# Scan steps, transpositions and layer 4 in another order in the second half of a macaron block

## What is computed

```python
x = x + 0.5 * ffn(layernorm(x))        # first half
x = x + attn(layernorm(x))             # a recurrence in place of attention
x = x + 0.5 * ffn(layernorm(x))        # second half, the same weights

def ffn(x):                            # widths 128, 512, 512, 512, 128
    h = silu(x @ w1.T * s1) * (x @ w2.T * s2)
    h = gelu(h @ h1.T * t1)
    h = gelu(h @ h2.T * t2)
    return h @ w3.T * s3

def attn(x):                           # 16 states
    xB = x @ B
    h_t = tanh(xB_t + h_(t-1) @ A.T)   # scanned over 512 positions
    return (h @ C) @ W_out.T + b_out
```

## Time and profile before

| what | value |
|---|---|
| median of 3 runs | 382.91 us |
| the profiled execution | 382.39 us |
| its span (first to last instruction) | 380.4 us |
| TensorE busy | 373.4 us (98%) |
| VectorE, ScalarE, GpSimd busy | 280.2 (74%), 261.0 (69%), 177.6 us (47%) |
| TensorE's granted clock over the span | 0.996 |

### The profile page before, as it was taken

The page is one execution under the profiler, slowest core; times in us unless marked ns, Lnnn a source line. Parts: engine busy times, 40 slices in busy tenths (PEclk is TensorE's granted clock), DMA queues, the critical chain, the costliest instruction groups (busy, mean ns, idle before and its releaser), DMA issues.

```text
span 380.4 us, 6512 instructions
## 1 busy us (share of the span) xinstructions
PE 373.4 (98%) x1773; PEld 297.2 (78%) x1773; DVE 280.2 (74%) x711; ACT 261.0 (69%) x605; POOL 177.6 (47%) x161
## 2 busy tenths in 40 slices
PE   7999999999999999999999999999999999999995
PEld 6877777878788787878778788888888888887774
DVE  5978988887787977677968876767867677786713
ACT  3889485667758678675684767858576785857653
POOL 2645265575746558342452623535233353533421
PEclk9999999999999999999999999999999999999998
DMA  7920010102001020000001000010100001010001
GB/s 235 434 108 1 28 57 28 57 2 83 3 28 56 2 83 0 28 1 29 28 2 55 3 28 28 2 55 1 55 0 27 28 0 55 0 52 7 2 28 32
DMA packets 7805, 16.64 MB, mean 44 GB/s; under 512 B 1888, under 2 KB 2912, under 8 KB 7520
## 3 DMA queue, kind: packets, MB, share of 16 engines
q1 hardware_dynamic: 6768, 16.01, 11.2%
q10 hardware_dynamic: 1008, 0.29, 0.3%
HBM read 9.99 MB, written 2.12 MB: 32 GB/s over the span
## 4 chain that ended last, share of the span: by engine, by line
PE 96%; ACT 2%; issue 0%; DVE 0%
PE F L288 75%; PE FR L288 8%; PE SC L504 2%; PE FR L316 1%; PE F L541 1%; PE SC L436 1%; PE F L532 1%; PE MI L316 1%; PE MI L296 1%; PE FR L306 1%; PE SC L288 1%; PE F L534 1%; PE SC L451 1%; ACT y_hi L1235 1%; PE MI L458 0%
## 5 line engine op out<-in xcount | busy, mean ns | idle before, releaser
L288 PE MATMUL F<-y_hi,w_hi 128*128 128x512 f32 (+1 forms) x484 | 196.9, 407 | 0.3 <-DVE y_lo L1059 0.2
L288 PE MATMUL F<-y_lo,w_hi 128*128 128x512 f32 (+1 forms) x484 | 188.4, 390 | 0.0
L288 PEld LDWEIGHTS F<-y_hi,w_hi 128*128 128x128 f32 x484 | 91.0, 188 | 24.0 <-issue 6.0
L1232 ACT ACTIVATE y<-F,sc 128x512 f32<-128x512 f32 x111 | 76.0, 685 | 43.1 <-PE F L288 41.9
L288 PEld LDWEIGHTS F<-y_lo,w_hi 128*128 128x128 f32 x484 | 91.2, 188 | 15.3
L853 DVE TENSOR_TENSOR y_lo<-y,y_hi 128x512 fp32r<-128x512 f32 x79 | 66.3, 839 | 39.9 <-ACT y_hi L1235 39.9
L1506 POOL TENSOR_TENSOR y_lo<-y,y_hi 128x512 fp32r<-128x512 f32 x48 | 66.6, 1394 | 58.7 <-DVE y_hi L840 48.1
L1512 POOL TENSOR_TENSOR y_lo<-y,y_hi 128x512 fp32r<-128x512 f32 x48 | 62.5, 1309 | 35.1 <-ACT y_hi L1235 35.1
L1235 ACT ACTIVATE y_hi<-F,sc 128x512 fp32r<-128x512 f32 x111 | 75.9, 684 | 0.0
L1251 ACT ACTIVATE h<-SC 128x32 fp32r<-128x32 f32 x96 | 18.8, 195 | 49.3 <-PE SC L451 48.3
L288 PE MATMUL F<-xn_hi,w_hi 128*128 128x512 f32 x118 | 49.4, 419 | 0.0
(11 more groups left out here) (177 smaller groups left out, 438.8 us busy)
## 6 DMA issues: line engine op xcount, KB each, us to landing
w_raw<-mr_row SPq DMA_DIRECT2D x5, 512.0 KB, 3.4
x_all<-in_xT SPq DMA_DIRECT2D x1, 2048.0 KB, 16.2
x_all<-x1c SPq DMA_DIRECT2D x8, 256.0 KB, 2.3
x_all<-lnin SPq DMA_DIRECT2D x8, 256.0 KB, 2.2
out<-outb SPq DMA_DIRECT2D x7, 256.0 KB, 2.0
x_all<-in_xtok SPq DMA_DIRECT2D x1, 1536.0 KB, 12.1
w_raw<-in_h1T SPq DMA_DIRECT2D x2, 512.0 KB, 7.7
w_raw<-in_h2T SPq DMA_DIRECT2D x2, 512.0 KB, 9.0
```

The costliest lines, as they stand in the source:

```text
L288: mm = nc.tensor.matmul(out, wtile(w, layer, k, m), y, start=first and i == 0, stop=last and i == len(pairs) - 1)
L1232: nc.scalar.activation(y23[:, m, :], bankt[:, :], ACT.Gelu, scale=s)
```

## The change

It moves calls within three streams. On TensorE, `middle_turn` has steps 3, 4, 6 and 7 of the second pass at other products of layer 3. `turn` has step 0 inside layer 4, `front_tokens` one product ahead of layer 4's end, step 1 ahead of layer 2 block 1, step 2 and `to_features` inside layer 2 block 2, step 3 ahead of layer 2 block 3, and step 5 behind layer 1 block 2 instead of ahead of it. For this `layer4` takes a function that it calls behind each product, and its signal is given inside the loop. VectorE and ScalarE get the steps 0 to 3, `front` and the low part of layer 2's block 1 in an order that follows. ScalarE's part from step 4 on stays as it was; so do GpSimd and SyncE.

```diff
--- before.py
+++ after.py
@@ -383,7 +383,7 @@
                         mm.then_inc(l3_mm, 1)
                     beside(k)
 
-            def layer4(g, gen):
+            def layer4(g, gen, beside=lambda k: None):
                 if isinstance(g, int) and g == 0:
                     pe.wait_ge(y3_hi_r, 3)
                 else:
@@ -395,7 +395,9 @@
                     else:
                         pe.wait_ge(y3_lo_dve, (KT - 1) * g + k)
                     mm = split_mm(B4[:, :], 4, k, 0, y3_hi[:, k, :], y3_lo[:, k, :], k == 0, k == KT - 1, gen)
-                mm.then_inc(l4_mm, 1)
+                    if k == KT - 1:
+                        mm.then_inc(l4_mm, 1)
+                    beside(k)
 
             def last_layer3(g, ms, ks, gen):
 
@@ -624,11 +626,11 @@
                 layer3(g, 0, gen, lambda k: x_times_b(mid) if k == 1 else step(0) if k == KT - 1 else None)
                 layer1(g + 1, 2, gen)
                 step(1)
-                layer3(g, 1, gen, lambda k: step(2 + k // 2) if k % 2 else None)
-                layer3(g, 2, gen, lambda k: step(4 + k // 2) if k % 2 else None)
+                layer3(g, 1, gen, lambda k: step(2) if k == 1 else None)
+                layer3(g, 2, gen, lambda k: step(3 + k // 2) if k % 2 == 0 else None)
+                step(5)
                 layer1(g + 1, 3, gen)
-                step(6)
-                layer3(g, 3, gen, lambda k: step(7) if k == 1 else None)
+                layer3(g, 3, gen, lambda k: step(6 + k // 2) if k % 2 == 0 else None)
 
             def last_turn(g, r, gen):
                 layer2(g, 0, gen, lambda i: layer4(g - 1, gen) if i == 2 else None)
@@ -648,28 +650,32 @@
                     if scan is not None:
                         scan_step(scan[0], scan[1], t)
 
-                def opening(i):
-                    if att is not None and i == 1:
+                def within_layer4(k):
+                    if k == 1:
+                        step(0)
+                    if k == 2:
+                        front_tokens(g + 1)
+
+                def opening(k):
+                    if att is not None and k == 1:
                         attention(att[0], att[1])
-                    if i == 2:
-                        if joined:
-                            layer4(g - 1, gen)
+                    if k == 2 and joined:
+                        layer4(g - 1, gen, within_layer4)
+                    if k == 2 and not joined:
+                        step(0)
                         front_tokens(g + 1)
                 layer2(g, 0, gen, opening)
-                step(0)
+                step(1)
                 layer2(g, 1, gen)
-                step(1)
-                layer2(g, 2, gen)
-                step(2)
-                to_features("f", xnt_f, FR, g + 1)
+                layer2(g, 2, gen, lambda k: step(2) if k == 0 else to_features("f", xnt_f, FR, g + 1) if k == 2 else None)
+                step(3)
                 layer2(g, 3, gen)
-                step(3)
                 layer1(g + 1, 0, gen)
                 layer1(g + 1, 1, gen)
                 step(4)
                 layer3(g, 0, gen)
+                layer1(g + 1, 2, gen)
                 step(5)
-                layer1(g + 1, 2, gen)
                 layer3(g, 1, gen)
                 step(6)
                 layer3(g, 2, gen)
@@ -1017,16 +1023,16 @@
                 if att is not None:
                     attention(att[0], att[1])
                 low1(g)
+                step(0)
                 front_stats(g + 1)
                 if joined:
                     layer4(1, g - 1, k - 1)
-                step(0)
                 step(1)
                 normalise("f", g + 1, FR, mv_f, rs_f, xnt_f)
+                step(2)
                 low(g, 1, y2_hi_r, y23, y2_hi, y2_lo, y2_lo_dve)
-                step(2)
+                step(3)
                 xn_low(g + 1)
-                step(3)
                 low(g, 3, y2_hi_r, y23, y2_hi, y2_lo, y2_lo_dve)
                 first_gates(g + 1, step, (4, None, 5, None))
                 step(6)
@@ -1350,12 +1356,11 @@
                 if scan is not None:
                     inject(scan[0], scan[1])
                 step(0)
+                step(1)
                 gelu2(g, 0)
-                step(1)
-                gelu2(g, 1)
-                step(2)
-                gelu2(g, 2, lambda: front(g + 1))
-                step(3)
+                gelu2(g, 1, lambda: step(2))
+                front(g + 1)
+                gelu2(g, 2, lambda: step(3))
                 gelu2(g, 3)
                 layer1(g + 1, 0)
                 layer1(g + 1, 1)
```

## The result

The changed kernel takes 388.99 us (median of 5 runs, 388.02 to 389.48) against 382.57 (5 runs, the three known before among them; 382.18 to 382.96): a ratio of 1.0171, interval 1.0156 to 1.0185. That is 1.1 us over the forecast of 387.9 and inside the range. Against the kernel before, 6.4 us were added where 5.0 were forecast: 1.4 more. The time misses by only 1.1 because the kernel before came out 0.34 lower than the 382.91 on which the forecast stood. The profiled executions are 389.48 us with a span of 387.4, and 382.39 with 380.4: 7.0 us apart, of which 0.4 arose before the middle turns, where the kernels are the same.

What follows compares the result with a forecast made beforehand. TensorE, 96% of the chain, was taken to bound the kernel. Loop turns 3.6, turn 1 0.6, turn 6 0.37 and middle turns 0.4 gave 5.0 on 382.39, 387.4; with 0.52 to the median, 387.9 us, range 383.7 to 389.6.

Steps and rivals of the forecast that it cites:

- the main term: Step 5 behind layer 1 block 2 delays `th`, the gate and layer 3 block 2: 0.49 us lost in each of five turns.
- A+3.46: TensorE's load for layer 3 block 2, 3.46 us after A, the start of layer 1 block 2; TensorE ready at A+2.98.
- the second transposition: On TensorE, waiting for `xnt_f` from VectorE and GpSimd: a loss between 0 and 0.23 us, taken as 0.10.
- layer 1 block 0: On TensorE, waiting for `xn_lo` behind step 3: 0.15 late plus 0.10 for the load, 0.25 us; 0.10 outside the loop.
- F+0.70: End of `xn_hi`, 0.70 us (0.66 and 0.04) after F, the second transposition, on the way to `xn_lo` at F+3.07.
- Turn 1: The turn whose waits use constants: losses 0.49, 0.10, 0.10 and 0.15 less 0.23 won, +0.6 us.
- Turn 6: Turn without scan: the chain to the second transposition starts 0.09 sooner, two matmuls (0.46) stand behind its end: +0.37 us.
- Middle turns: Steps 3, 6 and 7 win 0.15 us, step 5 loses 0.28: net +0.13, three times, 0.4 us.
- rival 3: ScalarE and VectorE don't catch up: `lnin` 0.2 later in five turns, attention waits 0.13 three times; +1.4, 389.3 us; chance 0.13.
- Rival 1: Faster: TensorE's queue swallows the short stops and only the old waits go, 381.3 us; chance 0.09.
- Rival 2: Only step 5's hold counts, 0.49 a turn in five turns less 1.6 won: 383.8 us; chance 0.13.
- Rival 4: Nothing happens, since the moved lines stand in turns that don't run: 382.9 us; chance 0.02.

Runs made afterwards that it cites:

- the first experiment: The changed kernel with scan step 5 ahead of layer 1 block 2 on TensorE again, all else as changed: 385.2 us, ratio 1.0079 to the kernel before.

## Why the prediction was right, and where its steps were off

**Right: the sign and the main term.** Step 5 holds ScalarE's `th`, that VectorE's gate, and that layer 3 block 2: 0.49 forecast, 0.47 + 0.02 measured, and of the forecast's "A+3.46" came A+3.47 (309.49 to 312.96); ScalarE's idling of "about 2 us" was 2.23, and turning ScalarE and VectorE round took the stall away. Layer 1 block 2 was 0.15 and is 0.17; the first transposition 0.14, and is 0.13; step 1 waits no longer; the middle turns' step 5 was 0.28 and is 0.29.

**Mis-sized: the second transposition**, 0.10 forecast, 0.22 measured, the upper bound of 0.23. The step that failed is "since step 1's `h` is out of the way": `xnt_f` idles 0.70 for GpSimd's `rs_f`, so VectorE's order ahead of it was no longer part of the way, and there was little to win by that. In the kernel before `rs_f` ended at 296.73, in the changed one at 300.81, and `xnt_f` follows that 0.13 later here; so step 1's `h` had held it by at most 296.95 - 296.86 = 0.09. The way took 302.31 - 297.37 = 4.94, the forecast's 4.96.

```profile
295.72 1.01 POOL L1501 TENSOR_TENSOR rs_f<-ve_f,mhalf 128x4 f32<-128x4 f32 x1 [0.16 <-POOL ve_f L1498]
...
299.80 1.01 POOL L1506 TENSOR_TENSOR rs_f<-ve_f,mhalf 128x4 f32<-128x4 f32 x1 [0.16 <-POOL ve_f L1503]
```

**Mis-sized: layer 1 block 0**, 0.25 forecast, 0.39 measured. Of "`xn_hi` at F+0.70" came F+0.78 (the 0.04 in it, for which the forecast shows no row, was 0.12); the way behind it (gelu 0.48, step 3 0.58, `h` 0.30, `xn_lo` 0.11 + 0.67) was right within 0.02 each, and 0.25 passed from its end to the load where I had 0.23. TensorE was there at F+2.89 instead of F+2.92. So 0.08, 0.02 and 0.03, all of one sign, made 0.13 of the 0.14: of a wait that is the difference of two long chains, small errors stay whole.

**Sums.** A loop turn was to cost 0.90 and cost 1.10 (1.12 in turn 4): these two terms are 0.26 more; the old waits give back 0.34 and not 0.23, but step 2 costs 0.09 more, which the forecast had at nothing; and the rest is within 0.02 each. Turn 1: 0.6 forecast, 0.94 measured; its first transposition waits 0.18, where I had 0, since `lnin` (226.22 + 0.75) ends 0.07 after TensorE gets there, and attention's wait for the middle turn's step 7, 0.12, falls into its start. Turn 6: 0.37 against 0.51: I had kept `lnin` in its place, but against the attention it ends 0.09 later than before (344.69 - 342.25 = 2.44, before 338.08 - 335.73 = 2.35), which takes the 0.09 that the chain to the second transposition was to win. Middle turns: 0.4 against 0.75: attention's wait (0.13 in rival 3, 0.12 measured) is real, and I had put it into a rival with a chance of 0.13 instead of the sum; two of the three fall into these stretches, the third into turn 1. And behind each middle turn VectorE is 0.3 late (`lnin` starts 1.62 after attention, 1.31 to 1.33 before). In the turns g = 7 and 8 layer 2 block 0 then waits 0.11 and 0.13 for the low part that VectorE makes behind `lnin` (in g = 7 it ends at 178.61, and the weight load is at 178.72); the forecast did not have this.

**Rivals.** Rival 1 (the queue swallows the stops) is out: the stops of turn 4 add to 1.38, 1.04 more than before, and the turn is 1.12 longer. The matmul behind a late load follows 0.33 or 0.34 after it in place of 0.228 (305.54 to 305.87, 309.49 to 309.83). The Trainium skill, "TensorE: Matmul & The Clock Gate", section "Part 2: What happens when you issue a matmul", has weight loads pulled ahead of matmuls in flight, by which that 0.10 would not be paid; the trace does not agree where the load itself stands behind a wait (load at 305.53, its matmul at 305.54). Rival 2 falls with the first experiment. Rival 3, whose 389.3 is nearer to the measured time than the forecast, was right in attention and in VectorE's delay behind the middle turns. Its larger term, `lnin` 0.2 later in five turns, is found in turn 1 alone: in turns 2 to 5 `lnin` starts at most 0.08 later after attention than before (in turn 4 1.31 in both kernels). So its near figure is in part luck. Rival 4 falls with the result. The rest of the 7.0 us is the 0.4 ahead of the middle turns, which no edit explains; over the profiles of all fourteen kernels x times B of g = 6 starts between 163.7 and 165.0 us, so it is within what differs from execution to execution.

## What to carry to other kernels

When a small step is moved on one engine, write down what stands behind it on each engine that follows it in the same order: here a scan step of 0.18 us held a `tanh`, a gate and a bank, and cost 0.65 a turn. Moving an operation earlier pays only if the chain that feeds it, and the one it feeds, move too; put a chain's members in the order in which TensorE wants them (`xn_low` ahead of step 3) and take other work, such as a low part, out of the way of the one that is late. Waits that only a rival has in the forecast but that have a definite price belong in the sum.

## What was not expected of the hardware

- A loop's turn-round costs VectorE 0.28 us of idling (292.12 to 292.40) behind a last instruction of 0.43; the same two instructions outside the loop follow each other at once, and with a low part of 0.69 at the loop's end it was covered. That it is the turn-round is inferred from these places; the waits in the loop also compare with register values, and no run separates the two.
- Two or three waits on register values that stand behind one that is late cost TensorE about 0.17 us together even if they are long satisfied (0.22 against 0.05 from value to load); where they compare with constants, putting the late one last did not help (0.05 against 0.11 to 0.12).
- The time outside the span, 1.9 to 2.1 us in nine of these twelve kernels, was 3.3 to 4.0 in the three whose first transposition looks at its late wait last. A gain in the span alone is therefore not yet a gain.
